# A graph kernel on one core: more dense blocks, fewer gathered groups, and two score banks for its units

## The reference, cut to what matters

```python
for _ in range(3):                                    # layer 1, "hops"
    msg = (x * norm_out[:, None])[src]
    agg = segment_sum(msg, dst, N)
    x = 0.5 * (agg * norm_in[:, None]) + 0.5 * h0
y = layernorm(h0 + x @ W0.T)
h = relu(concat([y[src], y[dst]], axis=1) @ W1 + b1)  # layer 2, "attention"
w = sigmoid(h @ W2 + b2)[:, 0]
attended = y + segment_sum(w[:, None] * y[src], dst, N)
out = layernorm(y + layernorm(attended) * gamma + beta)
```

## Time and profile before

| | us |
|---|---|
| three timed runs, median (lowest to highest) | 1120.77 (1120.27 to 1121.59) |
| the profiled execution | 1122.8 |
| its span, first to last instruction | 1121.1 |
| first hop | 212 to 315.6 |
| middle hop | 315.6 to 413.3 |
| last hop | 413.3 to 534.9 |
| first score product of unit 0 to that of unit 168 | 553.9 to 1070.2 |
| last norms | 1078 to 1121 |

### The profile page before, as it was taken

One profiled execution on the slowest core, in us unless ns is written; L12 is line 12 of the kernel. 1 busy time (PEld: TensorE's weight loads), 2 busy tenths in 40 slices (PEclk: granted clock), 3 DMA queues, 4 the chain that ended last, 5 costly groups with the idle time before them and its releaser, 6 DMA issues.

```text
span 1121.1 us, 33394 instructions
## 1 busy us (share of the span) xinstructions
PE 947.2 (84%) x11292; PEld 785.8 (70%) x11293; DVE 956.2 (85%) x2664; ACT 614.6 (55%) x1523; POOL 496.5 (44%) x676
## 2 busy tenths in 40 slices
PE   4889898787889888989479999999989999989950
PEld 2888888576677767777257787877767777777740
DVE  7999999589999998987479999998878888888866
ACT  6666776512100002222267777887767767767755
POOL 1000000300101003546777777777777777777711
PEclk9999999799999999999689999999989999999975
DMA  3000000000000000111476777777767776767601
GB/s 103 1 1 0 0 0 0 1 1 3 3 2 3 3 3 18 40 45 47 121 217 204 205 219 211 221 212 216 206 191 209 212 206 200 206 207 207 184 12 49
DMA packets 77517, 117.44 MB, mean 105 GB/s; under 512 B 20489, under 2 KB 38973, under 8 KB 77373
## 3 DMA queue, kind: packets, MB, share of 16 engines
q1 hardware_dynamic: 58172, 63.13, 18.8%
q0 software_dynamic: 19200, 52.45, 16.6%
HBM read 108.66 MB, written 6.86 MB: 103 GB/s over the span
## 4 chain that ended last, share of the span: by engine, by line
DVE 37%; POOL 26%; issue 16%; PE 15%; ACT 3%; DMA 1%; SPq 1%; DVEq 1%; ACTq 0%; POOLq 0%
POOL region L889 17%; POOL U L889 6%; PE bank L1772 5%; DVE stage L995 4%; DVE hx L995 3%; DVE aggT L1192 3%; DVE stage L1158 3%; DVE aggT L1167 2%; POOL stage L889 2%; DVE aggT L995 2%; DVE stage L1179 1%; DVE t L1251 1%; ACT region L2000 1%; PE bank L1869 1%; DVE t L1249 1%
## 5 line engine op out<-in xcount | busy, mean ns | idle before, releaser
L889 POOL DMA_INDIRECT region<-src_split,region x272 | 266.2, 979 | 84.8 <-issue 81.9
L1772 PE MATMUL bank<-U,region 128*128 128x256 f16 (+1 forms) x1875 | 236.8, 277 | 3.4 <-DVE U L1135 2.1
L1772 PEld LDWEIGHTS bank<-U,region 128*128 128x128 fp8e4 x1875 | 180.6, 99 | 37.3 <-DVE U L1135 2.8
L2186 ACT CAST region<-bank 128x512 f16<-128x512 f32 x338 | 180.7, 591 | 0.0
L2036 ACT CAST region<-bank 128x500 f32 x202 | 120.0, 594 | 56.0 <-PE bank L1661 46.6
L2166 ACT ACTIVATE region<-bank 128x512 f16<-128x512 f32 x169 | 100.9, 597 | 64.6 <-PE bank L1872 59.7
L1449 DVE SCALAR_TENSOR_TENSOR region<-bank,region 128x512 f16<-128x512 f32 x169 | 116.4, 688 | 15.9 <-ACT region L2166 12.4
L1869 PE MATMUL bank<-region,xs 128*128 128x256 f16 x676 | 106.0, 281 | 18.5 <-DVE region L1449 11.5
L1433 DVE TENSOR_SCALAR region<-region,stage 128x512 f16<-128x512 f16 x338 | 108.8, 363 | 9.8 <-DMA region<-slot_rows 9.8
L889 POOL DMA_INDIRECT U<-src_split,region x96 | 93.0, 969 | 29.3 <-issue 29.3
L1881 PE MATMUL bank<-U,region 128*128 128x256 f16 x676 | 105.9, 281 | 0.0
(11 more groups left out here) (293 smaller groups left out, 2320.2 us busy)
## 6 DMA issues: line engine op xcount, KB each, us to landing
region<-slot_rows SPq DMA_DIRECT2D x169, 256.0 KB
region<-in_dst_dram SPq DMA_DIRECT2D x100, 64.0 KB
region<-src_split,region POOLq DMA_INDIRECT x272
slot_rows<-aggT SPq DMA_DIRECT2D x104, 3.2 KB
src_split<-U SPq DMA_DIRECT2D x25, 64.0 KB, 1.5
src_split<-xs SPq DMA_DIRECT2D x25, 64.0 KB, 1.5
tgt_split<-q SPq DMA_DIRECT2D x25, 64.0 KB, 1.6
region<-tgt_split SPq DMA_DIRECT2D x100, 16.0 KB
```

Of the source, the lines that this page charges most:

```text
L889: nc.gpsimd.indirect_dma_start(out=rows_of(n, i), out_offset=None, in_=src_split, in_offset=bass.IndirectOffsetOnAxis(ap=listed[n % LISTS] ...
L1772: z = nc.tensor.matmul(bank[2 * (k % 2) + p][:, 0:width], count[:, h, b * P:(b + 1) * P], U[k % 2][:, h, 0:width], start=h == 0, stop=h == ...
L2186: nc.scalar.copy(y_rows[u % 4][:, a, :], bank[3 + a][:, :]).then_inc(rows_copied, 1)
```

## The change

- POOLED goes from 25 to 21, FIRST_BLOCK from 12 to 10: 84 batches over 186 steps, DENSE = 15 blocks, 30 half-blocks, 195 units, STEPS = 201.
- The half-blocks start by a new table: 10 in the first hop from step 3, 12 in the middle hop, 8 in the last. `count_earlier` runs a block later, and all that follows it too (numbers 4, places 5, fill 7, turn 8).
- A unit's slot list is stored twice, the second time with targets 64 higher (`upper_targets`, made by ACT), so each half of the partitions loads the list that fits it (two transfers of 128 KB), and `turn_pair` is one comparison of 1024 columns in place of two of 512.
- The scores of a unit and the z of its step share one bank, 5 or 6 by the parity of the step (`scores_in`). `fetch_pair` no longer waits for `pair_low`; it waits for `w_ready` of the step two before.
- `sum_pair` has the rows stationary and the weights moving: eight products of 128 and 64 columns in place of four of 256. The block's sums come out by feature, `copy_parts` copies 256 columns and not 512, `fold_parts` has two products and not four.
- SP issues the first slot loads ahead of the last block's table stores, and the first windows by halves in steps 2 to 5; the first units wait only for the source blocks that they use. The verdict on the inputs is put into bank 2 and is raised at step 8.

The core of the diff:

```diff
-    POOLED = 25
+    POOLED = 21
-    FIRST_BLOCK = 12
+    FIRST_BLOCK = 10
+    def scores_in(s):
+
+        return 5 + s % 2
...
+    SORTED_2, SORTED_3 = min(HALF_BLOCKS * 3 // 7, 12), 8
+    SORTED = ((HALF_BLOCKS - SORTED_2 - SORTED_3, 3, NB - 3), (SORTED_2, NB, NB), (SORTED_3, 2 * NB, NB - 7))
+
     def sorted_at(hs):
 
-        return 3 + hs * (2 * NB + 13) // (HALF_BLOCKS - 1)
+        for size, first, blocks in SORTED:
+            if hs < size:
+                return first + hs * blocks // size
+            hs -= size
...
+            def first_loads():
+                sp.wait_ge(hop_psum, 3 * NB)
+                sp.wait_ge(q_tabled[FIRST_BLOCK % 2], 16 * (FIRST_BLOCK // 2 + 1))
+                sp.wait_ge(slots_stored, STORED * HALF_BLOCKS)
+                load_slots(0)
+                targets_of(0)
+                load_slots(1)
+                load_slots(2)
...
             for c in range(NB + 2):
+                if c == NB + 1:
+                    first_loads()
                 tables(c, c % 2)
...
             def turn_pair(u):
-                dve.wait_ge(slots_loaded[u % 3], 16 * (u // 3 + 1))
+                dve.wait_ge(slots_loaded[u % 3], 32 * (u // 3 + 1))
                 if u >= 3:
                     dve.wait_ge(rows_psum, 2 * (u - 2))
-                for a in range(2):
-                    z = nc.vector.tensor_scalar(turned_hot[u % 3][:, a * 4 * P:(a + 1) * 4 * P],
-                                                slots_here[u % 3][:, a * 4 * P:(a + 1) * 4 * P],
-                                                row_no[:, a:a + 1], None, ALU.is_equal)
-                z.then_inc(turned_ready, 1)
+                nc.vector.tensor_scalar(turned_hot[u % 3][:, :], slots_here[u % 3][:, :], row_no[:, 0:1], None,
+                                        ALU.is_equal).then_inc(turned_ready, 1)
...
             def sort_products(s):
-                hs = sort_of(s, 2)
+                hs = sort_of(s, 3)
                 if hs is not None:
                     count_earlier(hs, s)
...
             def add_features(s):
...
-                if scored_steps(s) > 1:
-                    pe.wait_ge(w_ready, scored_steps(s) - 1)
+                if scored_steps(s - 2):
+                    pe.wait_ge(w_ready, scored_steps(s - 2))
...
             def fetch_pair(u):
...
-                if u:
-                    pe.wait_ge(pair_low, u)
+                if scored_steps(u + LEAD - 2):
+                    pe.wait_ge(w_ready, scored_steps(u + LEAD - 2))
+                scores = bank[scores_in(u + LEAD)]
...
             def sum_pair(u):
...
-                        z = nc.tensor.matmul(
-                            bank[7][:, t * 2 * D:(t + 1) * 2 * D],
-                            hot_weights[u % 3][:, 2 * i:2 * i + 2, :, t].rearrange("p a r -> p (a r)"),
-                            y_rows[u % 4][:, i, t * 2 * D:(t + 1) * 2 * D],
-                            start=m + i + t == 0, stop=m == UNITS - 1 and i + t == 2, skip_group_check=True)
+                        for y_half in range(2):
+                            z = nc.tensor.matmul(
+                                bank[7][:, t * P:t * P + (2 - y_half) * HD],
+                                y_rows[u % 4][:, i, (2 * t + y_half) * D:(2 * t + y_half + 1) * D],
+                                hot_weights[u % 3][:, 2 * i:2 * i + 2 - y_half, :, t],
+                                start=m + i + t + y_half == 0, stop=m == UNITS - 1 and i + t + y_half == 3,
+                                skip_group_check=True)
...
             def copy_lists(hs, s):
...
+                nc.scalar.activation(upper_targets[64 * t:64 * t + BUCKETS, i, :], here[0:BUCKETS, 0:P], ACT.Identity,
+                                     bias=half_offset[0:BUCKETS, 0:1])
```

More of the change, by code:

```diff
@@ L182, in gnn_kernel @@
         ohT = [carve(region, taken, [BE], f16) for _ in range(2)]
-        qwin = [carve(region, taken, [2 * D], f16) for _ in range(2)]
+        qwin = [sb(f"qwin{i}", [P, 2 * D], f16) for i in range(2)]
         ohJ = [carve(region, taken, [TPS // 2, JW, 2], f16) for _ in range(2)]
@@ L635, in _, with targets_of, load_slots @@
               .then_inc(w_loaded, 16)
+            def targets_of(i):
+                here = (FIRST_BLOCK + i) * P
+                if i >= 2:
+                    sp.wait_ge(pair_psum, (i - 1) * UNITS)
+                for half in range(2):
+                    sp.dma_start(q_pair[i % 2][half * HD:(half + 1) * HD, :, :],
+                                 tgt_split[here:here + P, half * D:(half + 1) * D]
+                                 .rearrange("(a r) k -> r a k", a=2)).then_inc(q_loaded[i % 2], 16)
+            def load_slots(u):
+                i, m = divmod(u, UNITS)
+                if u >= 3:
+                    sp.wait_ge(turned_ready, u - 2)
+                for h in range(2):
+                    sp.dma_start(slots_here[u % 3][h * HD:(h + 1) * HD, :],
+                                 slot_rows[i, m:m + 1, h, :].broadcast_to([HD, 8 * P])).then_inc(slots_loaded[u % 3], 16)
+            def first_loads():
[6 more added lines that the diff above has]
+                load_slots(2)
             def store_slots(hs):
@@ L1868, in fetch_pair @@
                     for half in range(2):
-                        nc.tensor.matmul(bank[5][:, a * 2 * P:(a + 1) * 2 * P], p_table[:, h, half * D:(half + 1) * D],
+                        nc.tensor.matmul(scores[:, a * 2 * P:(a + 1) * 2 * P], p_table[:, h, half * D:(half + 1) * D],
                                          turned_hot[u % 3][:, a * 2 * P:(a + 1) * 2 * P], start=a + half == 0, stop=False)
@@ L1902, in fold_parts @@
                 pe.wait_ge(parts_copied, i + 1)
-                for half in range(2):
-                    for a in range(2):
-                        z = nc.tensor.matmul(bank[2][:, P:2 * P], fold[:, (1 - half) * HD:(1 - half) * HD + P],
-                                             att_parts[:, (2 * half + a) * D:(2 * half + a + 1) * D],
-                                             start=half + a == 0, stop=half + a == 2)
+                for part in range(2):
+                    z = nc.tensor.matmul(bank[2][:, P:2 * P], att_parts[:, part, :, :].rearrange("p t r -> p (t r)"), ident[:, :],
+                                         start=part == 0, stop=part == 1)
                 z.then_inc(parts_folded, 1)
@@ L1927, in _ @@
                     sums((b - 3) // BPS, (b - 3) % BPS, blocks_folded(s - 1))
-                if s == 2:
+                if s == 6:
                     pe.wait_ge(chain["verdict"], 7)
-                    nc.tensor.matmul(bank[7][0:1, 0:3], one[:, :], verdict_sums[:, :], start=True, stop=True)\
+                    nc.tensor.matmul(bank[2][0:1, 0:3], one[:, :], verdict_sums[:, :], start=True, stop=True)\
                       .then_inc(verdict_psum, 1)
```

150 lines of the change are left out of this document (68 added, 82 removed).

## The result

The changed kernel takes 1209.05 us (median; 1206.36 to 1211.90) beside 1120.52 for the kernel before on the same chip: a ratio of 1.0791, 95% interval 1.0763 to 1.0819. Timed once more it took 1210.17, ratio 1.0769 (1.0746 to 1.0791). The forecast was 1191, slower.

The account below looks back on a forecast made before the run. The prediction took DVE as the bound of the hops and the gather as the pace of attention. Stage +60, sorting +16, start -5 and tail -1 gave +70 on 1120.8, so 1191 us, own range 1158 to 1216.

Parts of the forecast that it names:

- The loop: Attention stage: score product, relu, two row copies, two sigmoids, release, next score product; 2.89 us against 2.32.
- F: Start of a unit's first score product on PE in attention; forecast to follow the previous one by 2.89 in unit-only steps.
- The stage: Attention, first F to last F: forecast 575.9 us against 516.3, so +60 (bounds +45 to +70).
- the pair: Attention: a batch step plus a unit-only step, forecast 2.89 + 2.98 = 5.87 us against 5.38.
- the saving in the bucket sums: Attention, PE: narrower bucket-sum products save 0.08 us per unit (bounds 0 and 0.2), making unit-only to batch 2.98.
- The sorting: Hops: four more half-blocks cost +24 unabsorbed; DVE's waits could take up part, so +16 (bounds +4 and +25).
- rival B: Attention: PE's clock falls as PE idles; one pair in ten slow adds 34, giving 1225 us; chance 0.06.
- Start: Before the first unit: slot loads issued sooner bring its F forward, -5 us (bounds 0 and -6).
- tail: After the last F: final fold with four passes, -1 us; fewer blocks in the last group, bounds 0 and -4.
- A: Attention: the banks decouple and PE sets the pace; stage 480, -36, total 1095 us; chance 0.12.
- its point of decision: Attention: A needs the sigmoids to end less than 1.9 us after F; they end at 2.74.
- C: Attention: no change, as the gather waits that go pay for the longer loop; chance 0.02.

Follow-up runs that it names:

- e1: The changed kernel with ACT's two sigmoids of the step before moved ahead of the two row copies: 1129.92 us, ratio 1.0073.
- e2: As e1, and on PE the z products of the step before issued ahead of the unit's row products: 1124.43 us, ratio 1.0027.
- e6: The changed kernel with the old bank use, one bank for unit scores and another for z: 1155.18 us, ratio 1.0294.
- e3: The changed kernel with the old sorting lags, counting product two blocks after the scan, all behind it one block earlier: 1250.95 us, ratio 1.1155.
- e9: The kernel before with only the counting product and all that follows it one block later: 1122.45 us, ratio 1.0003.
- e4: The changed kernel with the old balance, POOLED 25 and FIRST_BLOCK 12 (13 dense blocks, 25 gathered groups): 1133.10 us, ratio 1.0111.

## Why the prediction was right, and where it was off

**The loop: right, and shown.** The sentence "F of step s no longer waits for the remainder of unit s-1, but for the sigmoids of step s-2" is what PE's wait for L2199 shows, and 2.89 was forecast where 2.88 came. e1 and e2 move the sigmoids, e6 takes the bank away, and 79, 84 and 53 us of the stage come back.

**The stage: +53 for +60.** The mis-sized term is the pair, 5.87. From the unit-only step to the next batch step it takes 2.93, not 2.98: the saving in the bucket sums is what I took, 0.08 (eight in 0.52, four in 0.60), but I took it from one distance of 3.06, and 49 of the 168 distances of before are about 3.01. A pair is 5.81, and 84 x 0.06 is 5 of the 7. Six steps have a fold that shows, five of 3.45 to 3.46 and one of 3.25 in place of 2.93; together they cost 3.0, for 3.8. No wait of ACT for batch scores exceeds 1 us, and the gathers pause, both as said.

**The sorting: the failed step.** "Four more half-blocks cost +24 if nothing absorbs it" was right: DVE's work grew by 26.0. What failed is "at most about 20 can be filled" of DVE's waits. The waits I counted were not spare time: over the three hops waits of those kinds went from 23.1 to 22.0 us, and two new ones came on top, 9.4 for the fill and 5.2 for ACT's copies of P. So idle time rose by 13.6 where I had let it fall by 8. The wait for the fill comes where the fill is a block later, which I read only as a gain, and half-blocks are closer, which I didn't look at: from 2.52 blocks to 2.1 to 2.25. The later counting product hangs on the spacing too. "Takes PE's wait for the scan away" was the smaller wait; the move also shortens that for the numbers, and is worth 41 us at the new spacing (e3) and nothing at the old one (e9). And the clock: I put its fall as rival B into attention, where it stayed at 0.99, and it fell in the hops; how much of the 13.6 that is stays open.

**Start, tail.** -3.3 for -5: the first slot load is issued 11.5 us behind the hops (585.20), 14.7 in before, as tables still stand ahead of it on SP. The tail gained 5.0, past its bound of 4; e4 has 49.8, so the fold gives the 1.0 that I took, and the balance gives the other 4.

**The rivals.** A did not come because the diff does not move the sigmoids; e2 shows that its point of decision (the sigmoids ending 1.9 after F) was right, e1 and e2 that its stage was near (490 and 485 for 480). C is refuted by e4 and e6: the gathers' waits would have paid for the longer loop only at the old balance.

**The time** came out 18 us above the forecast: 23.6 too little for the hops and 0.9 in the start, less 7.0 too much for the stage and 4.0 too little for the tail's gain; the other 4.5 are the median, which lies that much above the span of the profiled run. The misses are of both signs, so the total is nearer than its largest term.

## What to carry to other kernels

A second buffer helps only if its release comes earlier than that of the first; find the last reader of each buffer in its engine's program order, and move that reader forward before adding the buffer. An idle engine in a stage that another engine fills is not room for more work by itself: see what new waits the work brings, which buffer it takes and when that is handed back, how far apart the pieces stand, and where in the other engine's step each result comes. A part that is hidden by a slower one (the loop beside the gathers) must be priced again when the slower one is made faster.

## What the hardware showed that I had not expected

After a stop of PE of 3.06 us in a hop the granted clock fell to 0.57 in the next 6 us, and the same twenty products took 2.30 in place of 1.3 us. The pauses of 0.79 in the attention stage left it at 0.99. In e3, where the stops are longest, it was 0.85 and 0.91 over two whole hops of 130 us. And the same kernel's hops differed by 4 us between two profiles (362.4 and 366.5), with DVE's work the same to 0.2.
